# A map of their own for 24 tiles of the second expert stage, and the order of shared and routed tiles

## What is computed

```
x = x + attention_0(layernorm(x), ctx)
x = x + experts_0(layernorm(x))          # 8 experts, F = 512, top 2
x = x + attention_1(layernorm(x), ctx)   # rotary, window of 64
h = layernorm(x)
x = x + experts_1(h)
# experts_1, for each token t:
scores = softmax(h @ gate_w.T); idx = top_2(scores + gate_b)
expert(h) = silu((h @ w1 + b1) * (h @ w3 + b3)) @ w2 + b2     # 176 wide
y = sum over the two chosen of scores[e] * expert_e(h) ; z = shared_expert(h)
experts_1(h) = y + z
```

## Time and profile before

| | |
|---|---|
| three runs | 758.09, 761.66, 762.01 us; median 761.66 us |
| the profiled execution | 763.85 us, its span 762.0 us |
| busy: TensorE, VectorE, GpSimd, ScalarE | 667.7, 545.3, 500.1, 410.8 us |
| mean granted clock of TensorE | 0.954 of full |
| second attention loop and its tail | until about 618 us |
| first and last send of the second expert stage | 642.42 and 736.33 us |

### The profile page before, as it was taken

The page is one execution under the profiler, slowest core; times in us unless marked ns, Lnnn a source line. Parts: engine busy times, 40 slices in busy tenths (PEclk is TensorE's granted clock), DMA queues, the critical chain, the costliest instruction groups (busy, mean ns, idle before and its releaser), DMA issues.

```text
span 762.0 us, 20655 instructions
## 1 busy us (share of the span) xinstructions
PE 667.7 (88%) x6884; PEld 560.4 (74%) x6884; DVE 545.3 (72%) x1634; ACT 410.8 (54%) x1054; POOL 500.1 (66%) x850
## 2 busy tenths in 40 slices
PE   6599999988798999799998999999998779999950
PEld 4477777766567989799985777777776569999950
DVE  3579999999842674244425889999998667888735
ACT  2246555555554333234415777777775657777740
POOL 5354488788764897578745553777877762888850
PEclk9799999999999999899997999999999999999985
DMA  8192000000104522322211100111001133333229
GB/s 233 45 375 52 5 27 26 27 30 31 36 33 108 158 58 75 110 72 68 72 57 53 29 17 28 44 41 54 24 27 33 36 105 83 104 103 104 76 80 288
DMA packets 60988, 57.69 MB, mean 76 GB/s; under 512 B 11347, under 2 KB 54006, under 8 KB 60342
## 3 DMA queue, kind: packets, MB, share of 16 engines
q1 hardware_dynamic: 52246, 38.41, 18.0%
q0 software_dynamic: 8640, 17.97, 6.9%
HBM read 33.77 MB, written 22.08 MB: 73 GB/s over the span
## 4 chain that ended last, share of the span: by engine, by line
POOL 26%; PE 26%; DVE 22%; issue 16%; DMA 4%; ACT 2%; SPq 2%; POOLq 1%; DVEq 0%
POOL results L1353 9%; PE S L1770 6%; POOL rows L533 5%; DVE mx L908 5%; DVE pr L909 5%; PE ptp L1789 4%; PE S L1095 3%; POOL xi L1346 3%; PE S L1097 3%; POOL rstd L471 2%; PE M L1128 2%; DVE stats L789 2%; DMA results<-early,xi 2%; PE ptp L1113 2%; PE ptp L1067 2%
## 5 line engine op out<-in xcount | busy, mean ns | idle before, releaser
L533 POOL DMA_INDIRECT rows<-out_rows,posi x128 | 127.5, 996 | 47.9 <-issue 28.7
L672 ACT ACTIVATE pT<-ptp 128x512 f32<-128x512 f32 (+1 forms) x192 | 94.3, 524 | 101.6 <-PE ptp L1113 90.4
L908 DVE TENSOR_REDUCE mx<-S 128x16 f32<-128x1232 f32 x64 | 91.2, 1425 | 15.1 <-PE S L1097 14.4
L1353 POOL DMA_INDIRECT results<-early,xi x71 | 75.1, 1058 | 35.7 <-DVE early L1416 29.2
L909 DVE TENSOR_TENSOR pr<-S,mx 128x1232 f32<-128x1232 f32 x64 | 92.2, 1441 | 2.2
L1640 POOL DMA_INDIRECT results<-early,xi x71 | 70.4, 991 | 25.5 <-DVE early L1716 13.2
L1442 PE MATMUL S<-early,w1s 128*128 128x128 f32 x568 | 76.5, 278 | 3.8 <-DVE w1s L1409 3.0
L1452 PE MATMUL S<-first_w,early 128*128 x568 | 76.9, 279 | 0.8 <-DVE early L1416 0.7
L1128 PE MATMUL M<-pT,vm 128*32 128x128 f32 (+1 forms) x2048 | 70.3, 278 | 6.3 <-POOL vm L495 6.3
L1416 DVE TENSOR_SCALAR early<-S,xs 128x128 f32<-128x128 f32 x71 | 24.8, 349 | 69.2 <-PE S L1452 61.4
L1442 PEld LDWEIGHTS S<-early,w1s 128*128 128x128 f32 x568 | 69.9, 194 | 5.2 <-issue 4.4
(11 more groups left out here) (190 smaller groups left out, 1581.4 us busy)
## 6 DMA issues: line engine op xcount, KB each, us to landing
xs<-rows SPq DMA_DIRECT2D x142, 66.0 KB, 1.8
first_w<-in_e_W SPq DMA_DIRECT2D x2, 2048.0 KB, 10.8
swap<-results SPq DMA_DIRECT2D x32, 128.0 KB
first_w<-results SPq DMA_DIRECT2D x6, 512.0 KB, 7.2
results<-early,xi POOLq DMA_INDIRECT x142, 2.4
rows<-out_rows,posi POOLq DMA_INDIRECT x128, 2.3
W1r<-in_e_W SPq DMA_DIRECT2D x1, 1536.0 KB, 15.3
out_x<-x_res SPq DMA_DIRECT2D x3, 512.0 KB, 6.4
```

The costliest lines, as they stand in the source:

```text
L533: nc.gpsimd.indirect_dma_start(rows[:, :], bass.IndirectOffsetOnAxis(posi[:, k, n:n + 1], 0), out_rows[:, ring_slot(groups, n), k, :], Non ...
L672: nc.scalar.activation(pT[0:rows_of, G * r:G * r + count, :], ptp[q % 2][0:rows_of, 0:count, :], ACT.Exp, scale=SCALE)\
L908: do(V.tensor_reduce(mx[:, :].rearrange("p (g j) -> p g j", g=G), sc, AX.X, ALU.max))
L1353: nc.gpsimd.indirect_dma_start(results[:, :], bass.IndirectOffsetOnAxis(xi[:, s:s + 1], 0), ys[:, s, :], None)\
```

## The change

- Behind the products of attention steps k = 25, 26 and 27 VectorE makes in three parts (`early_map`) the map of the first 24 tiles. They are tiles that the rows of batches 0 to 15 fill completely: the counts after 4 groups are shifted right by 7. The first part has seven instructions, the second four on 24 x 7 elements, the third five and a wait for the first `maps_done`.
- The late map covers the other 47 tiles, starts behind those of the early map, and has three small instructions more; it makes `maps_done` 2.
- SHARED_FIRST goes from 22 to 16: by the diff the units are 8 shared pairs (16 batches), 36 routed units, 8 shared pairs (16 batches).
- SP waits for the early map and for the scatters of groups 0 to 3, issues 16 loads, then the fills, then loads 16 to 23, then waits for the full map, all scatters and the fills, and issues the others. The lanes of groups 6 to 8 are numbered so that each lane's first group is one of groups 0 to 3.
- TensorE waits for the early map ahead of the first routed unit, and for the full one ahead of tile 24.
- GpSimd's `note` and `xi` are gone: a send reads its indices from `xs` itself. Load i in its place waits until the send of tile i - 16 has landed.
- `x_done` counts the added halves, and up to four of them may come in the loop, from unit ADDS_FROM = 8 + 36 + 7 = 51 on.

```diff
-SHARED_FIRST = 22
+SHARED_FIRST = 16
+EARLY, EARLY_GROUPS, EARLY_AT = 24, 4, 24
+ADDS_AFTER, HALVES_EARLY = 7, 4
...
+        def early_map(part):
...
+            full, cu, eb = st["full"], st["full_u"], st["early_big"]
+            slot, by, of = cst[:, C_SLOT:C_SLOT + EARLY], *slots_of(EARLY)
+            if part == 0:
+                do(V.tensor_tensor(full[:, 0, :], carry[:, EARLY_GROUPS % 2, :], cst[:, C_FIRST:C_FIRST + E], ALU.subtract))
+                do(V.tensor_copy(cu[:, 0, :], full[:, 0, :]))
+                do(V.tensor_scalar(cu[:, 1, :], cu[:, 0, :], 7, None, ALU.logical_shift_right))
+                do(V.tensor_copy(full[:, 0, :], cu[:, 1, :]))
+                do(V.tensor_tensor_scan(full[:, 1, :], st["one"][:, :], full[:, 0, :], 0.0, ALU.mult, ALU.add))
+                steps.mark(V.tensor_scalar(full[:, 2, :], full[:, 1, :], float(EARLY), None, ALU.min))
+                do(V.tensor_scalar(full[:, 0, :], full[:, 0, :], -128.0, float(REGION), ALU.mult, ALU.add))
+            if part == 1:
+                do(V.tensor_tensor(eb[:, 0, :, 0:E - 1], by(slot), of(full[:, 1, 0:E - 1]), ALU.is_ge))
+                steps.mark(V.tensor_reduce(st["early_slot"][:, 0, :], eb[:, 0, :, 0:E - 1], AX.X, ALU.add))
+                do(V.tensor_tensor(eb[:, 1, :, 0:E - 1], eb[:, 0, :, 0:E - 1], of(full[:, 0, 0:E - 1]), ALU.mult))
+                do(V.tensor_reduce(st["early_slot"][:, 1, :], eb[:, 1, :, 0:E - 1], AX.X, ALU.add))
+            if part == 2:
+                steps.mark(V.tensor_copy(st["emap"][:, 0:EARLY], st["early_slot"][:, 0, :]))
+                do(V.scalar_tensor_tensor(st["early_slot"][:, 1, :], slot, 128.0, st["early_slot"][:, 1, :], ALU.mult, ALU.add))
+                V.tensor_copy(st["rowmap"][:, 0:EARLY], st["early_slot"][:, 1, :]).then_inc(maps_done, 1)
+                steps.mark(V.tensor_scalar(st["first128"][:, :], full[:, 2, 0:1], 128.0, None, ALU.mult))
+                steps.mark(V.tensor_tensor(full[:, 0, 0:E - 1], full[:, 2, 1:E], full[:, 2, 0:E - 1], ALU.subtract))
+                dve.wait_ge(maps_done, 1)
...
+            if rope and EARLY_AT < k <= EARLY_AT + 3:
+                dve.wait_ge(products_taken, k + 3)
+                early_map(k - EARLY_AT - 1)
...
+        if rope:
+            full = st["full"]
+            do(V.tensor_tensor(tmap[:, 2, :], tmap[:, 2, :], full[:, 2, :], ALU.subtract))
+            do(V.scalar_tensor_tensor(tmap[:, 3, 0:E - 1], full[:, 0, 0:E - 1], 128.0, tmap[:, 3, 0:E - 1], ALU.mult, ALU.add))
...
+    def early_rows(sp):
+
+        for g in range(EARLY_GROUPS):
+            sp.wait_ge(scattered[lane(groups, g)], 32 * in_lane(groups, g))
...
     def load(sp, i, row=None):
 
-        s, r = i % XU, (i - XU) // 2
+        s, before = i % XU, i - XU
         if i >= XU:
-            sp.wait_ge(xsT_ready, r + 1)
-            sp.wait_ge(xi_copied, r + 1)
-            sp.wait_ge(ys_ready, i - XU + 1)
+            sp.wait_ge(xsT_ready, before // 2 + 1)
+            sp.wait_ge(ys_ready, before + 1)
+            sp.wait_ge(ys_out[before % U], 16 * (before // U) + 16)
...
-        def note(r):
...
         def send(i):
 
-            s = i % U
+            s, place = i % U, xs[:, i % XU, IDX:IDX + 1].bitcast(U32)
+            in_place(pool, i)
             pool.wait_ge(ys_ready, i + 1)
-            pool.wait_ge(xi_copied, i // 2 + 1)
-            nc.gpsimd.indirect_dma_start(results[:, :], bass.IndirectOffsetOnAxis(xi[:, s:s + 1], 0), ys[:, s, :], None)\
-                .then_inc(ys_out[s], 16)
...
+            nc.gpsimd.indirect_dma_start(results[:, :], bass.IndirectOffsetOnAxis(place, 0), ys[:, s, :], None).then_inc(ys_out[s], 16)
...
+            if u - 2 >= ADDS_FROM and halves < HALVES_EARLY:
+                dve.wait_ge(z_ready, pairs_through(u - 3))
+                add_results(halves)
+                halves += 1
...
+            a1["early_set"](sp)
+            a1["early_rows"](sp)
+            for i in range(min(16, EARLY)):
+                e1["load"](sp, i)
+            a1["fill_up"](sp, range(E - 1, -1, -1))
+            for i in range(16, EARLY):
+                e1["load"](sp, i)
+            a1["maps_set"](sp)
+            a1["rows_landed"](sp)
+            for i in range(EARLY, SLOTS):
                 e1["load"](sp, i)
```

More of the change, by code:

```diff
@@ L421, in rows_in_place, with rows_landed @@
         maps_set(sp)
-        row = first_row(sp)
+        row = first_row(sp) if first_row else None
+        rows_landed(sp)
+        return row
+    def rows_landed(sp):
         rows_scattered(sp)
         sp.wait_ge(filled, 16 * E)
-        return row
     def first_loads(sp):
@@ L921, in normalise, with slots_of, by_slot, by_expert @@
                 ALU.mult, ALU.mult).then_inc(norm_done, 1)
+        def slots_of(size):
+            def by_slot(a):
+                return a.unsqueeze(2).broadcast_to([128, size, E - 1])
+            def by_expert(a):
+                return a.unsqueeze(1).broadcast_to([128, size, E - 1])
+            return by_slot, by_expert
+        def early_map(part):
[21 more added lines that the diff above has]
+                dve.wait_ge(maps_done, 1)
         steps.mark(V.tensor_copy(carry[:, 0, :], cst[:, C_FIRST:C_FIRST + E]))
@@ L1257, in maps_set, with early_set @@
     def maps_set(eng):
+        eng.wait_ge(maps_done, 2 if rope else 1)
+    def early_set(eng):
         eng.wait_ge(maps_done, 1)
+    def early_rows(sp):
+        for g in range(EARLY_GROUPS):
+            sp.wait_ge(scattered[lane(groups, g)], 32 * in_lane(groups, g))
     def x_updated(dve, n):
@@ L1478, with gated_experts @@
 ROUTED_AT = SHARED_FIRST // 2
-def gated_experts(nc, st, w, maps_set, x_updated, shared_turned):
+ADDS_FROM = ROUTED_AT + len(range(0, SLOTS, 2)) + ADDS_AFTER
+def gated_experts(nc, st, w, early_set, maps_set, x_updated, shared_turned):
     U = 8
@@ L1730, in add_results @@
             steps.then(dve, V.tensor_tensor(xb, xb, yg[:, 0, b0:b0 + HU, :], ALU.add))
-            V.tensor_tensor(xb, xb, yg[:, 1, b0:b0 + HU, :], ALU.add).then_inc(z_ready, 1)
+            V.tensor_tensor(xb, xb, yg[:, 1, b0:b0 + HU, :], ALU.add).then_inc(x_done, 1)
         dve.wait_ge(st["w1_less"], E)
+        halves = 0
         for u in range(NU + 2):
@@ L1741, in vector @@
                 results_of(u - 2)
+            if u - 2 >= ADDS_FROM and halves < HALVES_EARLY:
+                dve.wait_ge(z_ready, pairs_through(u - 3))
+                add_results(halves)
+                halves += 1
             yield u
         dve.wait_ge(z_ready, pairs_through(NU - 1))
-        for half in range(B // HU):
+        for half in range(halves, B // HU):
             add_results(half)
@@ L1798, in tensor @@
             if u >= ROUTED_AT and is_routed(u + 2):
+                if UNITS[u + 2][1] == EARLY:
+                    maps_set(pe)
                 take(u + 2)
@@ L1905, in build @@
                                    "results": results[0], "prefetch": []})
-        e1 = gated_experts(nc, st, {**w1, "rows": rows[1], "results": results[1]}, a1["maps_set"], a1["x_updated"], a1["shared_turned"])
+        e1 = gated_experts(nc, st, {**w1, "rows": rows[1], "results": results[1]}, a1["early_set"], a1["maps_set"], a1["x_updated"], a1["shared_turned"])
         def run(part):
@@ L1942, in _ @@
             run(a1["sync"](sp))
-            row = a1["rows_in_place"](sp, e1["first_row"])
-            e1["load"](sp, 0, row)
-            for i in range(1, SLOTS):
+            a1["early_set"](sp)
[8 more added lines that the diff above has]
+            for i in range(EARLY, SLOTS):
                 e1["load"](sp, i)
```

50 lines of the change are left out of this document (21 added, 29 removed), and 2 rows, old and new, of the table GROUPS_AT.

## The result

The changed kernel takes 759.22 us (median of 20 runs, 757.05 to 762.07), the kernel before 760.94 (20 runs): a ratio of 0.9975, 95% interval 0.9963 to 0.9986, or 1.9 us less (1.1 to 2.8). Forecast were 5.4 less.

A forecast was written before the change was run, and what follows sets the result against it. GpSimd's sends, 2.68 us a pair, were taken to bound the second expert stage. Span 762.0 - 5.9 + 3.7 + 0 - 3.5 + 0.3 = 756.6 us, 756.3 against the median; own range 753.5 to 759.5, wider range 752.5 to 762.

The forecast's parts named there:

- rival A: GpSimd's sends: their pace does not improve without the index copy; 759.5 us, chance 0.17.
- The start: Handover to routed units: with three shared pairs moved behind, first routed products and first send come 5.9 us earlier.
- The early map: VectorE in attention steps 25 to 27: the inserted instructions are paid in full, +3.7 us (bounds 2.5 and 4.5).
- Rows there in time: First routed units: 16 early loads, issued some 50 us ahead, cost nothing; without that cover 3 to 5 us.
- The index copy: GpSimd's sends: dropping the copy takes a pair from 2.68 to 2.58 us, -3.5 us (bounds 0 and -5.3).
- The load's new wait: Loop of sends, loads, TensorE and VectorE: 16.5 us fit into 15 sends, 19.4 us, so 0 for GpSimd.
- Rival B: Load's new wait: the loop closes, a waiting take delaying the older unit's product; +11.5 us, 767.8, chance 0.09.
- The end: Behind the last send: VectorE's adds of halves about level with the transfers of results, +0.3 us.
- Rival C: Attention loop: GpSimd's chain partly covers the map, 2.5 us or less remain; 755 us, chance 0.18 together with faster sends.
- Rival D: Attention loop: VectorE's insertions idle TensorE and its clock falls, 1 to 2.5 us; 758.5 us, chance 0.1.
- Rival E: First send: an early load or map entry is late and the send stays where it was; 761.9 us, chance 0.04.

The follow-up runs named there:

- e4_copy_kept: The changed kernel with the index copies back and load i waiting for them again, not for a send's landing: 759.66 us, ratio 0.9987.
- e1_more_buffers: The changed kernel with 24 row buffers instead of 16, so load i waits for the send of tile i - 24: 755.34 us, ratio 0.9924.
- e9_take_behind: The changed kernel with TensorE's transpose for unit u+2 put behind the second product of unit u-2: 754.62 us, ratio 0.9916.

## Why the prediction was wrong

Its direction was right, its size was not: -5.4 us forecast, -1.9 measured. 759.22 lies inside its range, 753.5 to 759.5, and next to the 759.5 of rival A, but for another reason. It is above 757.9, so by the prediction's own bounds the outcome is "same", which had 0.32 against 0.58 for faster.

*The start* (-5.9) **held** together with the map, within what executions differ by: from k = 25 to the first routed products 86.25 became 84.27, -2.0 us, where -5.9 + 3.7 = -2.2 were forecast. The three other kernels with the same map and order take 83.06 (`e4_copy_kept`), 84.94 (`e1_more_buffers`) and 85.11 us (`e9_take_behind`). This pair of executions has +3.7, -0.8 and -4.9 in its three parts; since the -0.8 isn't shown to be an effect, the -4.9 says little against -5.9. The first send lost a further 0.5, which lies between the result and a send that reads its index itself; this term was missing.

*The early map* (+3.7) **held** to 0.1 us: 22.03 - 18.30 = 3.73 in the changed kernel, 3.8 in the map alone, and 3.6 back when it is moved.

*Rows there in time* (0) **held**: no take of the first units waits for a load.

*The index copy* (-3.5) **was a little small**: 1.342 became 1.281 without the waits (-4.2 us), and 1.276 and 1.273 where the loop is open (-4.6 and -4.8). The surplus of 0.05 a pair, which I carried over, mostly goes away: the shortest possible pitch is 0.96 + 0.30 = 1.26. Rival A is out. The rule of the Trainium skill, page "SBUF — State Buffer", section "SBUF: two separate sides", would have kept the surplus and is not seen here: VectorE copies weights at an unchanged rate beside sends that take 0.96 us, so this case's trace does not show GpSimd locked out by them.

*The load's new wait* (0) **is the step that failed**. The prediction reckoned the way round over the 16 row buffers and asked whether 16.5 us fit into 15 sends, 19.4 us. It even wrote down what is queued behind a waiting take, the second product of an older unit, and did not ask what that product is due for. That product's send comes seven sends behind the one that the load waits for: 8.8 us of budget, of which the usual way takes 7.9. A margin of 2.9 us was in truth 0.9, and a send that lands after about 4 us instead of 2.3, or a load after 3.8 instead of 1.9, exceeds it. It cost 4.5 us in the profiled execution; exchanging the two steps in the queue gave 70 intervals of 89.1 us instead of 94.2 and brought the time down by 0.0059 of 761, 4.5 us, which by the two intervals is good to about 2 us and includes the 0.57 of the earlier first send.

Rival B named this mechanism, the waiting take that delays the older unit's product, but put it into the long way round: 2.6 us for each of 4.4 rounds. It happened four times in 71 tiles, at 1.1 us each. The condition was wrong as well: it needed no longer way round, just one late landing. It had a chance of 0.09 and the price of 11.5 us, both because it was measured against 15 sends.

*The end* (+0.3): +0.6, with the adds level with the transfers, as forecast (one wait of 0.47 us).

*Rival C*, a covered map: out. *Rival D*, a falling clock: from 583 to 587 it was 1.00 instead of 0.57 in the changed kernel's execution, but 0.50 in that of `e9_take_behind`, with the same map in the same steps. So this clock differs between executions, and neither a loss nor a gain by it is shown: the four kernels with this map and order take 84.3 us in the mean from k = 25 to the first routed products, where the forecast makes it 86.25 - 2.2 = 84.05, and D's 1 to 2.5 us are not in it. The Trainium skill, page "TensorE: Matmul & The Clock Gate", part 1, names the same two levels; the trace agrees with 0.50 and 1.00. *Rival E*, a first send that stays: out, it came 1.5 us sooner behind k = 25 (92.66 instead of 94.14).

With the failed term at its measured +4.5, the pace at -4.2 and the first send's +0.5, the sum is -5.9 + 3.7 + 0.5 - 4.2 + 4.5 + 0.3 = -1.1 us, at the edge of the measured interval, 1.1 to 2.8 less.

## What to carry to other kernels

When a wait closes a ring of buffers, the ring has not one way round but as many as there are things queued behind each waiting instruction; the budget is that of the shortest, counted in the steps of the engine that sets the pace, and it must hold the late landing, not the usual one. An instruction that may wait belongs behind everything in its queue that is ready and that others need. Work put into a stretch where one engine has no idle time cost its full length here: move it to where that engine waits anyway, and look at what it meets.

## What the runs showed of the hardware

The sends of 128 rows by an indirect DMA land in 2.2 to 2.3 us mostly, but up to 4.3 (3.9, 4.2 and 4.5 in other kernels). The DMA engines are busy only 0.30 to 0.38 of their time there, and no run shows what delays the late ones. In the traces of the ten kernels on the chips where the kernel before takes 761 us, sends that land after more than 2.9 us have no more weight copies of VectorE beside them (0.30 us in the mean) than those that land within 2.5 us (0.31). Loads of the same rows take 1.9 us in the median, and the one in the chain above 3.81. A plan by medians left 0.9 us of room, and that was not enough.

The kernel before took 761 us on two chips and 816 on a third, 7% more, with equal busy times of VectorE, ScalarE and GpSimd. In the expert stage the difference is pauses of 2 to 3.4 us in the hand-overs between engines, about every 7 to 8 us. What causes them stays open, also whether it is the chip. The ratio of the changed kernel to the kernel before was not taken there; that of the exchanged steps was 0.9956 instead of 0.9916.
